# First layer of a graph network: ScalarE in half groups, VectorE's additions ahead of its comparison

## The reference, cut to what matters

```
m = relu(feat[src]) + 1e-7
ex = exp(m - seg_max[dst])
msg = segment_sum(ex / segment_sum(ex, dst)[dst] * m, dst)
x = layernorm(x + (feat + msg) @ W + b)
```

## Time and profile before

| | |
|---|---|
| median of 3 runs | 4349.58 us (4344.03 to 4349.85) |
| the profiled execution's own time | 4346.85 us |
| its span in the trace | 4345.4 us |
| POOL busy | 3281.0 us (76%) |
| PE busy | 2864.4 us (66%) |
| DVE busy | 2149.3 us (49%) |
| ACT busy | 832.6 us (19%) |
| first layer's gathers begin, end | 2.9 us, about 2186 us |
| second layer's gathers begin | 2219.2 us |

### The profile page before, as it was taken

One profiled execution on the slowest core, in us unless ns is written; L12 is line 12 of the kernel. 1 busy time (PEld: TensorE's weight loads), 2 busy tenths in 40 slices (PEclk: granted clock), 3 DMA queues, 4 the chain that ended last, 5 costly groups with the idle time before them and its releaser, 6 DMA issues.

```text
span 4345.4 us, 46774 instructions
## 1 busy us (share of the span) xinstructions
PE 2864.4 (66%) x13152; PEld 2540.4 (58%) x13152; DVE 2149.3 (49%) x5595; ACT 832.6 (19%) x1958; POOL 3281.0 (76%) x3330
## 2 busy tenths in 40 slices
PE   3555555555555555555567878877778877877876
PEld 3444444444444444444457777777677777777776
DVE  6444444444444444444445555555555555555555
ACT  1222222222222222222211111111111111111111
POOL 7777777777777777777757777777777777777776
PEclk8666665767656765667767676667766677677676
DMA  4222222222222222222234444444444444444443
GB/s 107 43 43 44 47 45 43 43 43 49 43 43 43 44 48 43 43 44 49 43 86 129 130 129 128 129 128 130 128 128 127 130 128 130 130 128 130 130 130 104
DMA packets 289435, 376.50 MB, mean 87 GB/s; under 512 B 153301, under 2 KB 195958, under 8 KB 289174
## 3 DMA queue, kind: packets, MB, share of 16 engines
q0 software_dynamic: 132864, 245.03, 23.6%
q1 hardware_dynamic: 156310, 128.41, 10.6%
HBM read 353.82 MB, written 19.32 MB: 86 GB/s over the span
## 4 chain that ended last, share of the span: by engine, by line
POOL 75%; issue 23%; PE 0%; DVE 0%; DMA 0%; ACT 0%; POOLq 0%; SPq 0%; DVEq 0%; ACTq 0%
POOL rows L417 75%; PE banks L504 0%; DMA rows<-key_value,src_i 0%; PE banks L482 0%; DMA rows<-in_x,src_i 0%; DMA key_value<-qkv 0%; DMA src_i<-in_src 0%; DVE outs L874 0%; DVE vals L938 0%; DVE merged L806 0%; PE banks L473 0%; POOLq L65 0%; PE banks L465 0%; DVE prod L932 0%; DVE bn L858 0%
## 5 line engine op out<-in xcount | busy, mean ns | idle before, releaser
L417 POOL DMA_INDIRECT rows<-in_x,src_i x1661 | 1677.6, 1010 | 506.4 <-issue 505.7
L417 POOL DMA_INDIRECT rows<-key_value,src_i x1661 | 1602.0, 964 | 538.8 <-issue 505.6
L504 PE MATMUL banks<-ex,onehot 128*128 128x192 f32 x3322 | 1029.1, 479 | 966.3 <-issue 740.3
L504 PEld LDWEIGHTS banks<-ex,onehot 128*128 128x128 f32 x3322 | 860.1, 287 | 1125.2 <-issue 1120.7
L882 DVE SCALAR_TENSOR_TENSOR ex<-relu,ex 128x384 f32<-128x384 f32 x416 | 231.4, 556 | 1175.2 <-ACT ex L654 1175.0
L932 DVE TENSOR_TENSOR prod<-rows,banks 128x384 f32<-128x384 f32 x416 | 230.1, 553 | 963.9 <-DMA rows<-key_value,src_i 959.2
L536 PE MATMUL banks<-we_sb,ea 97*128 97x96 f32 x3322 | 642.9, 357 | 0.0
L536 PEld LDWEIGHTS banks<-we_sb,ea 97*128 97x128 f32 x3322 | 593.1, 267 | 0.0
L567 PEld LDWEIGHTS banks<-onehot,vals 128*104 128x104 f32 x3322 | 541.0, 252 | 2.3 <-DVE vals L938 2.3
L567 PE MATMUL banks<-onehot,vals 128*104 128x64 f32 x3322 | 538.0, 330 | 1.8 <-DVE vals L938 1.8
L556 PE MATMUL banks<-ident,onehot 128*128 128x128 f32 x832 | 246.7, 393 | 421.8 <-DVE onehot L780 418.9
(11 more groups left out here) (98 smaller groups left out, 1422.0 us busy)
## 6 DMA issues: line engine op xcount, KB each, us to landing
ea<-in_edge_t SPq DMA_DIRECT2D x415, 192.0 KB
rows<-in_x,src_i POOLq DMA_INDIRECT x1661, 2.5
rows<-key_value,src_i POOLq DMA_INDIRECT x1661
qw<-query SPq DMA_DIRECT2D x832, 24.0 KB
key_value<-qkv SPq DMA_DIRECT2D x24, 384.0 KB, 3.6
x<-in_x SPq DMA_DIRECT2D x7, 672.0 KB, 7.6
query<-qkv SPq DMA_DIRECT2D x24, 192.0 KB, 2.1
out<-outs SPq DMA_DIRECT2D x24, 192.0 KB
```

What stands on the lines that cost most here:

```text
L417: pool.indirect_dma_start(out=to[0:n, r, u, :], out_offset=None, in_=table, in_offset=bass.IndirectOffsetOnAxis(ap=src_i[0:n, g * G + u:g ...
L504: last = nc.tensor.matmul(ps_sum0[b], onehot[:, r, u, :], ex[:, b, u, :], start=u == 0, stop=u == n - 1)
```

## The change

ACT takes relu and exponential of a group in two halves of two tiles, each half waiting for its own two tiles; the exponential of a group no longer stands behind the relu of the next. For that each slot of the ring has two semaphores, one for each half. POOL's wait counts two relu instructions to a group, DVE's wait two exponentials. On DVE the additions come ahead of the comparison, which loses a wait that the additions already make.

```diff
-            def gather(g, r, to, table, s):
+            def gather(g, r, to, table, sems):
...
-                    ).then_inc(s, 16)
+                    ).then_inc(sems[u * len(sems) // G], 16)
...
-                    pool.wait_ge(s_relu, g - R0 + 1)
+                    pool.wait_ge(s_relu, 2 * (g - R0 + 1))
...
+                def half_tiles(g, h):
+                    return min(h * G // 2, tiles_of_group(g)), min((h + 1) * G // 2, tiles_of_group(g))
+
+                def relu_rows(g, h):
+                    b, r = g % 2, g % R0
+                    lo, hi = half_tiles(g, h)
+                    if hi == lo:
+                        return
+                    act.wait_ge(s_row[r][h], 16 * (G // 2) * (g // R0) + 16 * (hi - lo))
+                    if g >= 2 and h == 0:
                         act.wait_ge(s_p, g - 1)
+                    ins = nc.scalar.activation(relu[:, b, lo:hi, :], xr[:, r, lo:hi, :], ACT.Relu)
+                    ins.then_inc(s_relu, 1)
...
+                def exp_rows(g, h):
...
+                    act.wait_ge(s_relu, 2 * g + h + 1)
+                    if g >= 2 and h == 0:
                         act.wait_ge(s_sum, g - 1)
...
-                relu_rows(0)
                 for g in range(NG):
-                    if g + 1 < NG:
-                        relu_rows(g + 1)
-                    exp_rows(g)
+                    for h in range(2):
+                        relu_rows(g, h)
+                        exp_rows(g, h)
                     node_stages(g - 2)
...
-                    dve.wait_ge(s_exp, g + 1)
+                    dve.wait_ge(s_exp, 2 * g + (2 if n > G // 2 else 1))
...
                     if g < NG:
                         weigh_rows(g)
-                    if g + 2 < NG:
-                        if g >= 2:
-                            dve.wait_ge(s_sum, g - 1)
-                        make_onehot0(g + 2)
                     if g:
...
                         add_rows(g - 1, ats[k], ats[k + 1])
+                    if g + 2 < NG:
+                        make_onehot0(g + 2)
+                    if g:
                         node_stages(g - 1)
```

More of the change, by code:

```diff
@@ L165, in build @@
         s_wi = sem("s_wi")
-        s_row = [sem(f"s_row{r}") for r in range(R0)]
+        s_row = [[sem(f"s_half{r}_{h}") for h in range(2)] for r in range(R0)]
         s_relu = sem("s_relu")
@@ L434, in _ @@
                         pool.wait_ge(s_vals, g - R1 + 1)
-                    gather(g, g % R1, rows, key_value, s_row1[g % R1])
+                    gather(g, g % R1, rows, key_value, [s_row1[g % R1]])
                 pool.nop(nofuse=True)
@@ L641, in _ @@
             with act.If(1 - irregular(act, ACT_ENGINE)):
-                def relu_rows(g):
-                    b, r, n = g % 2, g % R0, tiles_of_group(g)
-                    act.wait_ge(s_row[r], 16 * G * (g // R0) + 16 * n)
-                    if g >= 2:
-                        act.wait_ge(s_p, g - 1)
[L647 to L652, removed]
+                def half_tiles(g, h):
[7 more added lines that the diff above has]
+                    if g >= 2 and h == 0:
+                        act.wait_ge(s_p, g - 1)
+                    ins = nc.scalar.activation(relu[:, b, lo:hi, :], xr[:, r, lo:hi, :], ACT.Relu)
+                    ins.then_inc(s_relu, 1)
+                def exp_rows(g, h):
+                    b = g % 2
+                    lo, hi = half_tiles(g, h)
+                    if hi == lo:
+                        return
+                    act.wait_ge(s_relu, 2 * g + h + 1)
+                    if g >= 2 and h == 0:
                         act.wait_ge(s_sum, g - 1)
-                    nc.scalar.activation(ex[:, b, 0:n, 0:D], relu[:, b, 0:n, :], ACT.Exp,
-                                         bias=gneg[:, :]).then_inc(s_exp, 1)
+                    ins = nc.scalar.activation(ex[:, b, lo:hi, 0:D], relu[:, b, lo:hi, :], ACT.Exp, bias=gneg[:, :])
+                    ins.then_inc(s_exp, 1)
                 def node_stages(at):
```

## The result

The changed kernel takes 4355.41 us (median of 18 runs, 4350.72 to 4360.04), the kernel before beside it on the same chip 4347.57 us. The ratio is 1.0018, with a 95% interval of 1.0011 to 1.0026: a small loss of 8 us, clear of the noise and within the 0.2% (8.7 us) that the prediction calls no change. The prediction was 4354.

The account below looks back on a forecast made before the run. POOL was taken to bound the kernel: 2 x 1661 gathers, each its duration and 0.30 us, and a 32.97 us gap. +9 + 6 - 6 - 5 = +4 us on the median 4349.58 gave 4354 us, range 4330 to 4380.

Parts of the forecast that it names:

- The bound: Whole kernel: time is a sum over POOL's gathers, each its duration and 0.30 us, plus a 32.97 us gap between layers.
- Part 1: ACT in halves: relu to product takes 0.88 us instead of 1.06, so the product comes 0.18 us earlier against POOL's gathers.
- Part 2: DVE's new order: one collision with a gather becomes two, +0.025 us a group, +9 us over some 365 regular groups.
- Part 3: First-layer groups out of step: those with table loads become regular, +6 us; those at a chunk's messages save 6 us.
- ties at a chunk's messages: DVE instructions starting almost with a gather, hoped to miss it: -13 us if all miss, 0 if lost, -6 taken.
- Part 4: Between the layers: the last full chunk's messages come a group earlier, so POOL's 32.97 us gap falls by about 5.
- The sum: First layer and gap together: +9 + 6 - 6 - 5 = +4 us, added to the median of 4349.58 us.
- The rule: A two-SBUF-input DVE instruction begun before a gather and running 0.125 us after its start delays it until that instruction ends.
- Slower halves: Rival, chance 0.2: ACT's halves save less, relu to product over 0.92 us; at 0.95, +30 us, 4380.
- the 3.7 us for each 0.01: Cost claimed for each 0.01 us more from relu to product, as both collisions end with the product's time.
- No second collision: Rival, chance 0.17: the comparison does not hold up a gather; -25 us, about 4325, at the far end 4279.
- Nothing but the gap: Rival, chance 0.13: POOL's excess stays as it was and only the join between layers saves 5 us: 4345.

Follow-up runs that it names:

- whole-groups run: Kernel after, but ACT in whole groups of four tiles, each exponential directly behind its own relu: 4351.1 us beside the kernel before's 4342.3, ratio 1.0019.
- the order alone: Kernel before with only DVE's new order (product, additions, comparison): 4413.3 us beside 4343.0, ratio 1.0154; where landings were late 5221.7 us, ratio 1.0032.
- PSUM runs: Kernel after with the first layer's comparison reading its 0..127 from PSUM: 4271.4 us beside the kernel before's 4342.3; where landings were late 5190.8 and 5144.4 us.
- the control: Kernel before with the comparison reading its 0..127 from PSUM instead of SBUF: 4339.1 us beside 4342.3, ratio 0.9995.

## Why the prediction was right

- *The bound.* POOL set the end before and after, and the 13.9 us of the first layer are the lengthening of its gathers: (1018 - 1010) x 1661 = 13.3.
- *Part 1.* Relu to product: 0.88 expected, 1000.68 to 1001.56 = 0.88 measured; halves of 363 and 455 ns expected, 362 and 454 measured. ACT's wait on its own relu, which had no row, is 1001.08 - 1001.04 = 0.04, not 0.03.
- *Part 2.* The comparison starts 1.33 behind the product (1.32 expected) and does not overlap the second addition, which ends at 1002.87. The Trainium skill's rule on instructions that start in another group of 32 partitions (VectorE: DVE Perf Modes, "Two Vector instructions with no wait between them") agrees: 1002.89. With 0.69 for its duration, where 0.68 was taken, it ends at 2.02 instead of 2.005. A gather of 1.04 and one of 1.15 were expected, 1.01 and 1.16 came. In the 320 groups clear of messages and table loads the mean excess is 0.278 us where it was 0.247 (medians 0.295 and 0.257): +0.031 instead of +0.025, +10 us where +9 was expected.
- *Part 3.* The groups with a table load became regular, as said. After:

```profile
786.85 1.28 ACT L664 ACT_TABLE_LOAD   x1
...
790.13 0.56 DVE L891 SCALAR_TENSOR_TENSOR ex<-relu,ex 128x384 f32<-128x384 f32 x1 [3.25 <-ACT ex L664]
790.50 1.01 POOL L417 DMA_INDIRECT rows<-in_x,src_i  x1 [0.30 <-issue]
```

The load is over before the second half's tile lands, and the gather that went free before now collides: +0.27 us x 23 = +6 (23 groups, not the 24 of the prediction). The ties at a chunk's messages were not won as hoped; after:

```profile
763.85 0.56 DVE L819 TENSOR_TENSOR merged<-merged,x 128x384 f32<-128x384 f32 x1
763.98 1.25 POOL L417 DMA_INDIRECT rows<-in_x,src_i  x1 [0.30 <-issue]
...
765.14 0.49 DVE L891 SCALAR_TENSOR_TENSOR ex<-relu,ex 128x384 f32<-128x384 f32 x1
765.53 0.94 POOL L417 DMA_INDIRECT rows<-in_x,src_i  x1 [0.30 <-issue]
```

The second product of the messages came 0.07 us earlier than before, nearly as expected (763.85 for 763.83), but POOL came 0.14 us later (763.98 for 763.84), through the two collisions of the group ahead, so this instruction began first and costs 0.31; the 0.48 of the earlier trace rows is gone. Over the three groups around each chunk's messages the excess went from 23.6 to 21.5 us in all: -2 us instead of -6. This is the term of the sum that was furthest off.
- *Part 4.* 27.67 us: -5.3, its bound; I took -5. The whole-groups run, with the new order and the lag gone but no halves, has the same 27.7, and the order alone 32.1, so it is the lag that held the gap.
- *The sum.* +13.9 - 5.3 + 2.1 + 0.4 = 11.1 against the predicted +4 for one execution, and 7.8 on the medians. Of the 7 us missed in the profiled execution, 4 are the messages', 2 the second layer's, which lie in its +-3, and 1 the regular groups'. That 4354 came within 2 us of 4355.41 is in part luck: the three runs that it was added to had a median 2 us above that of the 18 runs.
- *The rule.* As stated it does not cover a row that the prediction itself shows: the product of 765.21 began 0.12 behind its gather and held it up. That is the exception at a clearing, 12 of the 108 us of excess. Nor is it so that neither loses where the gather began first: there the gather keeps its time, but a product that began just behind it takes up to 0.59 us instead of 0.56. The sum took its 0.48 from the row itself, so neither slip is in it.
- *The rivals.* Slower halves: the durations excluded it, and the 3.7 us for each 0.01 do not hold as far as the whole-groups run. No second collision: 387 comparisons say otherwise. Nothing but the gap: refuted by the +13.9.

The Trainium skill's statement that VectorE's instructions with two SBUF inputs contend with GpSimd's reads (SBUF — State Buffer, "Who interferes with whom") agrees with the PSUM runs: all of the comparison's collisions, 81.6 us, gone with one input moved, and 3 us in the control. Its rule that the first comer keeps the ports for its whole instruction holds here for VectorE alone: the product of 1001.06 above began inside a gather and took 0.57 us instead of 0.56, where waiting for the gather's end would have cost it 0.9, and the most that any product beside a gather's start lost in the kernel before was 0.07.

## What to carry to other kernels

Where an engine of fixed rate sets the end, look for the instances of its instruction that are longer than the median, and at what else was running when they began: here 65 ns of mean over median hid 108 us. A change of order or of latency elsewhere then acts through phase, and both directions have to be worked out in each phase; a gain (66 us by the halves) and a loss (70 to 76 us by the order) can cancel to a change of 8 us. Here, taking the collision away by moving one input to PSUM was surer than steering past it, since a tie can go either way; but an edit that only moves an input can also move the instruction in time, so look for gathers that it still crosses before calling the input the cause.

## What the runs showed of the hardware

The margin of the tie is sharp. Of the products of the kernel before that were running at a gather's 0.125 us (those directly behind a clearing left out), the 348 that began 0.047 us or more ahead of it held it up until their end, and the 29 that began 0.042 us ahead or later did not at all. In the whole-groups run the border lies at 0.045. Such a tie is not free for VectorE: the product that began 0.042 ahead took 0.63 us instead of 0.56, those that began 0.04 or more behind took their 0.56. The additions, with one input in PSUM, lay across that point 376 times ahead of a gather without holding it up once.

Where landings are late the kernel before took 5203 us instead of 4343. No trace of those executions is kept, but the order alone has one there: 57 pauses of all transfers over 1.5 us long in its first 2 ms (332 us in all), against 3 in the kernel before's own profile by the same count. What causes them stays open.
